# Attention in half-precision pairs, with transposing DMAs for x and the gate weights

## What is computed

```python
def xattn(query, key, value, w_q, w_k, w_v, w_o):      # 16 heads of 64
    q, k, v = (split_heads(a @ w) for a, w in ((query, w_q), (key, w_k), (value, w_v)))
    scores = einsum('bhqd,bhkd->bhqk', q, k) * 64 ** -0.5
    scores = scores + (1.0 - mask) * -10000.0           # k_pos <= q_pos
    weights = softmax(scores)
    return merge_heads(einsum('bhqk,bhkd->bhqd', weights, v)) @ w_o

def ffn(x, w_gate, w_up, w_down):       # qdq: round to 16 bits, lpbq: to 4 bits in blocks of 32
    x = qdq(x)
    up, gate = qdq(x @ lpbq(w_up).T), qdq(x @ lpbq(w_gate).T)
    o = qdq(qdq(gate * qdq_u16(sigmoid(gate))) * up)
    return o @ lpbq(w_down).T

x = x + tanh(g_xattn) * xattn(layernorm(x), ctx, ctx, ...)
x = x + tanh(g_ffn) * ffn(layernorm(x), ...)
```

## Time and profile before

| | |
|---|---|
| median of the runs | 1377.19 us |
| profiled execution | 1376.84 us |
| its span (first to last instruction) | 1375.1 us |
| PE busy | 1267.9 us (92%) |
| DVE busy | 1008.5 us (73%) |
| ACT busy | 663.6 us (48%) |
| POOL busy | 238.4 us (17%) |

### The profile page before, as it was taken

The page is one execution under the profiler, slowest core; times in us unless marked ns, Lnnn a source line. Parts: engine busy times, 40 slices in busy tenths (PEclk is TensorE's granted clock), DMA queues, the critical chain, the costliest instruction groups (busy, mean ns, idle before and its releaser), DMA issues. The chain is left out here.

```text
span 1375.1 us, 19079 instructions
## 1 busy us (share of the span) xinstructions
PE 1267.9 (92%) x6157; PEld 754.2 (55%) x6157; DVE 1008.5 (73%) x1465; ACT 663.6 (48%) x782; POOL 238.4 (17%) x331
## 2 busy tenths in 40 slices
PE   7999999999999999999999999999990069999998
PEld 6778868878887864444444444444440024444443
DVE  0379778878967666777777499989999984555544
ACT  3434443343344224444443388857768973434331
POOL 1034324314423221111111032210210000000000
PEclk9999999999999999999999999999995579999999
DMA  8002212312212338776665799963377954545453
GB/s 335 2 24 96 82 46 85 99 38 77 92 69 69 103 135 253 223 225 217 214 214 164 237 323 339 332 226 138 130 259 296 322 193 133 181 154 185 157 171 112
DMA packets 126475, 231.95 MB, mean 169 GB/s; under 512 B 38352, under 2 KB 50640, under 8 KB 126416
## 3 DMA queue, kind: packets, MB, share of 16 engines
q1 hardware_dynamic: 126128, 231.26, 49.9%
q10 hardware_dynamic: 288, 0.00, 0.0%
HBM read 136.32 MB, written 91.23 MB: 165 GB/s over the span
## 5 line engine op out<-in xcount | busy, mean ns | idle before, releaser
L1799 PE MATMUL pD<-Wh,xph 128*128 128x512 f16 x384 | 145.5, 379 | 1.0 <-DVE xpl L1774 1.0
L1276 PE MATMUL gpG<-xph,Wh 128*128 128x512 f16 x384 | 145.8, 380 | 0.2 <-DVE xpl L1198 0.2
L1276 PE MATMUL gpG<-xpl,Wh 128*128 128x512 f16 x384 | 145.8, 380 | 0.0
L1276 PE MATMUL gpG<-xph,Wl 128*128 128x512 f16 x384 | 145.8, 380 | 0.0
L1276 PE MATMUL pU<-xph,Wh 128*128 128x512 f16 x384 | 145.5, 379 | 0.0
L1276 PE MATMUL pU<-xpl,Wh 128*128 128x512 f16 x384 | 145.5, 379 | 0.0
L1276 PE MATMUL pU<-xph,Wl 128*128 128x512 f16 x384 | 145.5, 379 | 0.0
L1799 PE MATMUL pD<-Wl,xph 128*128 128x512 f16 x384 | 145.5, 379 | 0.0
L1799 PE MATMUL pD<-Wh,xpl 128*128 128x512 f16 x384 | 145.5, 379 | 0.0
L1181 ACT ACTIVATE gst<-gpG,rw 128x512 f32<-128x512 f32 x96 | 65.8, 686 | 148.1 <-PE gpG L1276 144.4
L1211 DVE TENSOR_REDUCE gmx<-gst 128x512 f32 (+1 forms) x96 | 65.5, 682 | 61.9 <-ACT gst L1181 61.7
(11 more groups left out here) (223 smaller groups left out, 2608.9 us busy)
## 6 DMA issues: line engine op xcount, KB each, us to landing
dub<-up_d SPq DMA_DIRECT2D x42, 768.0 KB, 4.8
gate_d<-gst SPq DMA_DIRECT2D x96, 256.0 KB, 2.6
gb<-gate_d SPq DMA_DIRECT2D x24, 768.0 KB, 7.1
up_d<-ust SPq DMA_DIRECT2D x72, 256.0 KB, 5.3
eu<-up_d SPq DMA_DIRECT2D x22, 768.0 KB, 6.4
xr<-xn_d SPq DMA_DIRECT2D x9, 1024.0 KB, 6.5
xin<-in_x SPq DMA_DIRECT2D x32, 256.0 KB, 2.8
x_d<-x SPq DMA_DIRECT2D x32, 256.0 KB, 2.0
```

The costliest lines, as they stand in the source:

```text
L1276: mm = pe.matmul(ps[:, :], Ws[:, it, kt * P:(kt + 1) * P], xs[:, kt, :], start=(kt == 0 and Ws is Wh and xs is xh), stop=(kt == KT - 1 and ...
L1799: mm = pe.matmul(pD[4 * t + q][:, :], os_[n][:, cs], Ws[:, it, :], start=(it == 0 and os_ is oh and Ws is Wh), stop=(it == IT - 1 and os_ ...
```

## The change

All halves of attention become float16 in place of fp32r: xh, xl, Ah, Al, pTh, pTl, Vh, Vl. To stay in float16's range each operand is scaled: x by 2^10 and p by 2^14 with constants, A and V by factors from bounds that are computed once (the largest absolute values of w_q and kT, of w_o and vT, spread over the partitions by TensorE, `spread_bounds`, and worked on by VectorE in `fit_a` and `fit_v`); the factors are taken out again in the exp and in the residual.

x is no longer turned by TensorE. ACT rounds the normalised rows into nh, GpSimd subtracts into nl, and SP turns both by transposing DMAs into xh and xl, of which there are now four each, two steps before they are used. The gate weight jobs go the same way: ACT rounds the dequantised tile, GpSimd subtracts, SP turns both halves, and stores them one step later.

```diff
         xin = [sb(ph, f"xin{n}", [P, H], F32) for n in range(BQ)]
         xn = [sb(ph, f"xn{n}", [P, H], F32) for n in range(2)]
-        xh = [sb(ph, f"xh{n}", [P, H], F32R) for n in range(2)]
-        xl = [sb(ph, f"xl{n}", [P, H], F32R) for n in range(2)]
+        nh = [sb(ph, f"nh{n}", [P, H], F16) for n in range(2)]
+        nl = [sb(ph, f"nl{n}", [P, H], F16) for n in range(2)]
+        xh = [sb(ph, f"xh{n}", [P, H], F16) for n in range(4)]
+        xl = [sb(ph, f"xl{n}", [P, H], F16) for n in range(4)]
...
# SP, step
+                if have(k + 2):
+                    j = k + 2
+                    sp.wait_ge(*tile(xl_done, b, j))
+                    sp.sem_inc(J.apart, 1)
+                    sp.wait_ge(*tile(s_ps, b, j - 4))
+                    sp.sem_inc(J.apart, 1)
+                    for part_, to in ((nh, xh), (nl, xl)):
+                        sp.dma_start_transpose(blocks_of(to[j % 4]), part_[j % 2][:, :]).then_inc(xt_in[j % 2], 16)
+                q = job_at(k, jobs, 3)
+                if q is not None:
+                    dsts = job_dst(b, q)
+                    sp.wait_ge(*at(turn_in[q % 2], 16 * JB * b, 32 * (q // 2) + 32))
+                    sp.sem_inc(J.apart, 1)
+                    for part_, dst in zip(turned[q % 2], dsts):
+                        sp.dma_start(dst, part_[:, :]).then_inc(J.stored[q % 2], 16)
                 q = job_at(k, jobs, 2)
                 if q is not None:
-                    job_store(sp, J, b, q, job_dst(b, q))
+                    sp.wait_ge(*at(J.lo_done, JB * b, q + 1))
+                    sp.sem_inc(J.apart, 1)
+                    sp.wait_ge(*at(J.stored[q % 2], 16 * JB * b, 32 * (q // 2)))
+                    sp.sem_inc(J.apart, 1)
+                    for part_, to in zip((J.hi[q % 2], J.lo[q % 2]), turned[q % 2]):
+                        sp.dma_start_transpose(blocks_of(to), part_[:, :]).then_inc(turn_in[q % 2], 16)
                 q = job_at(k, jobs, 1)
                 if q is not None:
                     job_load(sp, J, b, q + J.NJ, job_src(b, q + J.NJ))
...
# GpSimd, step
+                q = job_at(k, jobs, 2)
+                if q is not None:
+                    n = q % J.NJ
+                    pool.wait_ge(*at(J.hi_done, JB * b, q + 1))
+                    pool.wait_ge(*at(turn_in[n], 16 * JB * b, 32 * (q // 2)))
+                    pool.tensor_tensor(J.lo[n][:, :], J.d[n][:, :], J.hi[n][:, :], ALU.subtract).then_inc(J.lo_done, 1)
                 if have(k - 1):
...
+                if have(k + 2):
+                    j = k + 2
+                    pool.wait_ge(*tile(xh_done, b, j))
+                    pool.wait_ge(*used(b, j))
+                    pool.tensor_tensor(nl[j % 2][:, :], xn[j % 2][:, :], nh[j % 2][:, :], ALU.subtract).then_inc(xl_done, 1)
...
# VectorE, step
                         for h, cs in enumerate(halves):
                             dve.wait_ge(*part(pTh_done, b, j, h))
-                            dve.tensor_tensor(pTl[:, cs], pT[:, cs], pTh[:, cs].bitcast(F32), ALU.subtract).then_inc(pTl_done, 1)
+                            dve.scalar_tensor_tensor(out=pTl[:, cs], in0=pT[:, cs], scalar=P_TOP, in1=pTh[:, cs],
+                                                     op0=ALU.mult, op1=ALU.subtract).then_inc(pTl_done, 1)
...
-                if have(k + 1):
-                    j = k + 1
-                    dve.wait_ge(*tile(xh_done, b, j))
-                    dve.wait_ge(*tile(s_ps, b, j - 2))
-                    dve.tensor_tensor(xl[j % 2][:, :], pX[:, :], xh[j % 2][:, :].bitcast(F32), ALU.subtract).then_inc(xl_done, 1)
...
+            for r in range(2):
+                dve.wait_ge(wq_in[r], 16)
+            largest_of(0, flat(wq))
             for j in range(2):
                 statistics(0, j)
+            dve.wait_ge(k_sb, ROUNDS)
+            largest_of(1, flat(kT))
+            dve.wait_ge(id_set, 2)
+            fit_a()
+            dve.wait_ge(wo_in, 16)
+            largest_of(2, flat(wo))
             schedule(dve, step, straight=True)
...
# TensorE
             def scores(b, k):
-                pe.wait_ge(*tile(xl_done, b, k))
+                pe.wait_ge(*at(xt_in[k % 2], 16 * BQ * b, 32 * (k // 2) + 32))
...
-                        for kt in range(KT):
-                            mm = pe.transpose(pX[:, kt * P:(kt + 1) * P], xn[j % 2][:, kt * P:(kt + 1) * P], ident[:, :])
-                        mm.then_inc(xT_ps, 1)
...
-                q = job_at(k, jobs, 1)
-                if q is not None:
-
-                    pe.wait_ge(*tile(xl_done, b, k + 1))
-                    job_turn(pe, J, b, q, ident)
```

More of the change, by code:

```diff
@@ L189 @@
 ROUNDS = 4
+X_TOP, P_TOP, M_TOP = 2.0 ** 10, 2.0 ** 14, 2.0 ** 15
 def four_tiles(xn_d, T):
@@ L412, in front_phase @@
         srec = sb(ph, "srec", [P, 2, HEADS], F32)
+        bounds = sb(ph, "bounds", [P, 4], F32)
+        wide = sb(ph, "wide", [P, 4], F32)
+        fit = sb(ph, "fit", [P, 16], F32)
+        (A_TOP, A_T, A_UNIT, A_INV, A_SCALE, S_UNIT, S_SCALE, V_TOP, V_T, V_UNIT, V_INV, V_SCALE, V_BACK, O_SCALE) = (
+            fit[:, n:n + 1] for n in range(14))
         pT = pb(ph, "pT", 1024)
@@ L417, in front_phase @@
         x1_out, x2_out, gate_stored = front_out
-        J = Jobs(mk, ph, "pj", JB, 2, [pX], gate_stored)
+        J = Jobs(mk, ph, "pj", JB, 2, None, gate_stored)
+        turned = [[sb(ph, f"pj{part}T{n}", [P, 512], F16) for part in ("hi", "lo")] for n in range(2)]
+        turn_in = [sem(f"pj_turn_in{n}", 32) for n in range(2)]
+        xt_in = [sem(f"xt_in{n}", 32) for n in range(2)]
         with ExitStack() as early:
@@ L443, in front_phase @@
         kbd_set, vb_set = sem("kbd_set"), sem("vb_set")
+        bound_done, bound_ps, fit_link, a_fit, v_fit = (sem(n) for n in ("bound", "bound_ps", "fit_link", "a_fit", "v_fit"))
         apart_p, apart_e = sem("apart_p"), sem("apart_e")
@@ L616, in normal, with high_rows @@
                 act.activation(to[n][:, :], src[:, :], ACT.Identity, bias=rs_[:, n, 2:3], scale=rs_[:, n, 1:2]).then_inc(done, 1)
+            def high_rows(b, j):
+                act.wait_ge(*tile(xn_done, b, j))
+                act.wait_ge(*used(b, j))
+                act.activation(nh[j % 2][:, :], xn[j % 2][:, :], ACT.Copy).then_inc(xh_done, 1)
             def step(b, k, have, jobs):
@@ L622, in step @@
                     of_batch(act, vT, vb, b + 1, vb_set)
-                q = job_at(k, jobs, 2)
-                if q is not None and which == 0:
-                    job_hi(act, J, b, q)
                 if have(k - 2):
@@ L630, in step @@
                         act.wait_ge(*part(pT_ps, b, j, h))
-                        act.activation(pTh[:, cs], pT[:, cs], ACT.Copy).then_inc(pTh_done, 1)
-                if q is not None and which != 0:
-                    job_hi(act, J, b, q)
+                        act.activation(pTh[:, cs], pT[:, cs], ACT.Copy, scale=P_TOP).then_inc(pTh_done, 1)
                 def chunk_high(n):
                     act.wait_ge(*at(ch_ps, NCH * b, NCH * ahead + 8 * which + n + 1))
+                    if not jobs and b == 0 and ahead == 0 and n == 0:
+                        act.wait_ge(v_fit if which else a_fit, 1)
                     if which == 0:
-                        act.activation(Ah[:, n // 2, halves[n % 2]], bank_of(k, 0, n), ACT.Copy, scale=SCALE).then_inc(ch_hi, 1)
+                        act.activation(Ah[:, n // 2, halves[n % 2]], bank_of(k, 0, n), ACT.Copy, scale=A_SCALE).then_inc(ch_hi, 1)
                     else:
-                        act.activation(Vh[:, block_of(n), :], bank_of(k, 1, n), ACT.Copy).then_inc(ch_hi, 1)
+                        act.activation(Vh[:, block_of(n), :], bank_of(k, 1, n), ACT.Copy, scale=V_SCALE).then_inc(ch_hi, 1)
                 early_highs = 2 if which == 0 and have(k - 2) else 0
@@ L654, in exponentials @@
                         act.wait_ge(*tile(sub_done, b, j))
-                        act.activation(pr[j % 2][:, :], pr[j % 2][:, :], ACT.Exp).then_inc(exp_done, 1)
+                        act.activation(pr[j % 2][:, :], pr[j % 2][:, :], ACT.Exp, scale=S_UNIT).then_inc(exp_done, 1)
                 def high():
-                    if have(k + 1):
-                        j = k + 1
-                        act.wait_ge(*tile(xT_ps, b, j))
-                        act.wait_ge(*tile(s_ps, b, j - 2))
-                        act.activation(xh[j % 2][:, :], pX[:, :], ACT.Copy).then_inc(xh_done, 1)
+                    if have(k + 2) and k + 2 >= 2:
+                        high_rows(b, k + 2)
+                    q = job_at(k, jobs, 1)
+                    if q is not None:
+                        n = q % J.NJ
+                        act.wait_ge(*at(J.deq_done, JB * b, q + 1))
+                        act.wait_ge(*at(turn_in[n], 16 * JB * b, 32 * (q // 2)))
+                        act.activation(J.hi[n][:, :], J.d[n][:, :], ACT.Copy).then_inc(J.hi_done, 1)
                 def normal2():
@@ L814, in normal @@
```

(16 more changed lines are left out.)

101 lines of the change are left out of this document (70 added, 31 removed).

## The result

The changed kernel takes 1364.84 us (median of 4 runs, 1361.4 to 1366.12) against 1376.93 beside it: ratio 0.991, 95% interval 0.9892 to 0.9927. It is faster by 12.1 us, where 28.6 were forecast; 1364.8 lies in the range, near its end. The execution that was profiled is the quickest of the four: 1361.4 us, span 1359.2.

A forecast was written before the change was run, and what follows sets the result against it. TensorE was taken as the bound, with VectorE full in job steps. Gains of 22.8 us in three job batches, 4.9 in the last, 0.9 before the first and 0 at the start sum to 28.6: 1349 us, range 1334 to 1366.

The forecast's parts named there:

- The plain step: A last-batch step (one tile of 128 rows) without weight jobs: from 12.42 to 11.45 us, not TensorE's own 11.2.
- the loop through the softmax: Chain from TensorE's start through ACT, VectorE and GpSimd's product to the next step's transposes: 11.4 us, not shortened.
- rival 2: GpSimd's subtraction of half-precision data nearer 1.9 us than 1.05, about 3 us a batch more: 1357 us, chance 0.17.
- the load's wait: VectorE waits 2 us, once in a batch, for job 3's weight tile, whose load SP issues later behind DMA transposes.
- steps 3 to 7: Tiles of 128 rows in a batch with weight jobs: 64.05 to 61.1 us, a gain of 3.0 a batch.
- the start: New reductions and small VectorE operations before the first steps: taken as 0, between a gain of 1 and a loss of 3.
- Steps 8, 9, 10: Last three steps of a job batch: step 8 gains 2.0 us, steps 9 and 10 together 2.6, their softmax loop having room.
- eight re-entries: Step 8: first matmul behind each fp32 product of A gets 0.1 us quicker, 0.7 in all.
- Steps with jobs: VectorE is the one that is full: VectorE works 13.17 us without pause, more than TensorE's 12.84; low halves leave it, so 12.0 in steps 4 to 6.
- rival 3: DMA transposes slow in traffic, both halves 10.5 us instead of 3.7, some 15 us back: 1363 us, chance 0.10.
- Rival 1: TensorE stays the only bound, as if VectorE, GpSimd and SP had room: gain 46, 1331 us, chance 0.12.
- Rivals 2, 4 and 5: 4: transposes landing past 10 us, slower, 1401 us, chance 0.05. 5: time goes elsewhere, nothing left, 1377, 0.04.

The follow-up runs named there:

- e6: Changed kernel with VectorE's residual ahead of the scores' maximum and subtraction in steps 3 to 6, its statistics behind the subtraction: 1357.36 us.
- e10: Changed kernel with the next weight tile's load ahead of x's transposes, ScalarE's output tile ahead of the weight's high half, and e6's order: 1348.39 us.
- e9: Changed kernel with all five moves: early load, output tile first, residual first with statistics last, block maxima in PSUM, tile 2's statistics earlier: 1337.08 us.
- e2: Changed kernel with SyncE issuing the load of the next weight tile ahead of x's transposes instead of behind them: 1357.31 us.
- e3: Changed kernel with the weight tile's block maxima kept in PSUM instead of SBUF: 1358.77 us.
- e11: Changed kernel with the early load of e2, ScalarE's output tile ahead of the weight's high half, and the block maxima of e3: 1348.56 us.
- e5: Changed kernel with the weight tiles turned by TensorE as before; half precision and x's turn by DMA stay: 1365.14 us.
- e4: Half precision alone: changed kernel with x and weights turned by TensorE as before and VectorE making the low halves from PSUM: 1365.77 us.
- e7: Changed kernel with tile 2's statistics on VectorE before the reduction of the last weights at the start: 1357.99 us.
- e12: Changed kernel with early load and output tile first, plus x's DMA transposes issued twice, the first pair into tiles nobody reads: 1360.35 us.
- e1: The changed kernel run again without any edit: 1362.92 us.

## Why the gain was less than half of the forecast

**What came as forecast.** TensorE: a half-precision matmul every 0.216 us, no turns. The plain step: 11.54 against 11.45, and the loop through the softmax sets it: with 0.9 us of VectorE taken from the loop (e6) it is 11.23, TensorE's own 11.2. The 0.09 over are the exp's, 1.15 us with its scale read from a tile, 1.06 before; an edit that I took at nothing. The last batch 4.7 against 4.9. The turns: 1.20 and 1.25 us of SP, landed in 2.5. GpSimd's subtraction 1.16 against 1.05, far from rival 2's 1.9; the load's wait 2.74 against 2.

**Where it went.** In the profiled execution 12.8 of the 28.6 us are missing: 5.1 in steps 9 and 10, 4.1 in steps 3 to 7, 2.2 in step 8 (each in three batches) and 1.4 at the start; the rest cancels. The median lacks 3.7 more, which no trace of its execution shows.

**The step that failed most: "Steps 8, 9, 10".** They hold 7.3 of the 12.8. Steps 9 and 10, forecast 28.2, were 29.9. "Their softmax loop has room in 8 and 9, and is met within 0.3 us in 10" was wrong in 9. Behind VectorE's subtraction comes ScalarE's exp, behind that its high half of V, behind that VectorE's low half, and for this TensorE waits 0.77 us (404.15). With the statistics out of that chain (e6, e10) the wait is gone and step 9 takes 15.72 instead of 16.56. Step 10 lost to something that the prediction didn't ask for, TensorE's wait of 0.49 us for the residual (415.74); without it (e6, e10) the step takes 12.86 instead of 13.34, and the two steps together 28.58. The other wait of step 10, 1.22 us for a low half of V, is 1.21 in e10 and is no part of this gain.

Step 8, 18.67 against 18.0, is the 0.7 for eight re-entries, a bound of 0 to 1.2 a batch of which the whole was taken. e9 has no pause in step 8, and 18.67 still. The matmuls of A in the kernel before, then in e9:

```profile
272.94 1.05 PE L891 MATMUL pT<-kbd,wqT 128*128 128x128 f32 x8
273.74 0.48 PE L925 MATMUL pO<-Vh,pTh 128*128 128x512 f32 x1
274.06 0.41 PE L925 MATMUL pO<-Vl,pTh 128*128 128x512 f32 x1
```

```profile
355.11 1.05 PE L1007 MATMUL pT<-kbd,wqT 128*128 128x128 f32 x8
356.00 0.38 PE L1041 MATMUL pO<-Vh,pTh 128*128 128x512 f16 x1
356.21 0.38 PE L1041 MATMUL pO<-Vl,pTh 128*128 128x512 f16 x1
```

The re-entry did come, 0.21 us to the next matmul instead of 0.32, but the eight products ahead of it take 0.89 instead of 0.80, and give it back. That term was put at nothing.

**"Steps with jobs: VectorE is the one that is full": the wrong reason, and near the right number by luck.** It took VectorE's 13.17 us for work, and each 0.6 taken from it for a gain. The earlier trace rows has no pause, but an instruction that is held counts as busy. The scaling had 0.85 us before, for a job that it does in 0.17 when nothing holds it. In the changed kernel it took 1.44 in steps 3 and 4, and VectorE's steps were 11.94 and 12.82 in the third batch (forecast 11.4 and 12.0); in 5 and 6, where GpSimd's new low half moved the product behind the scaling, it took 0.17 to 0.32, and VectorE's steps without the load's wait (e2) are 11.63 (forecast 12.0). What two steps lost the other two gained: the four take 48.0 us against 47.4. So against the forecast the held time cost little; what it could have given is 4 us, as e3 and e11 show. e5 shows the exchange one for one.

**The load** was the larger part of what steps 3 to 7 lost. With the load early (e2) they take 59.2, 59.8 and 59.5 us, against the forecast's 59.1 without the load's wait; in the changed kernel 61.8, 63.6 and 62.0. So the wait cost 2.6, 3.8 and 2.6 where 2 were forecast, the 3.8 in the batch where the clock fell behind the pause at 254.71. The prediction named "everything behind it in its order" behind the wait, and didn't follow it to TensorE: VectorE's residual stands there, and TensorE's value matmuls wait for residuals for 13 us in 12 places, 0.7 us before.

**The start**, forecast 0 between -1 and 3, cost 1.4. The new reductions (4.42 and 2.27 us against 4.8 and 2.4) come before tile 2's statistics, whose normalisation stands on ScalarE in front of A's first halves. e4 has the same late start (76.53) without any DMA turn: it belongs to the bounds. e7 gets 5.0 to 6.0 us of it back.

**Two ends of the sum.** Before the experiments the change read as half precision plus turns by DMA. e4 and e5 say which part paid: by the ratios, 10.7 of 14.0 us are half precision; the turn of x by DMA added 0.5 and the weights' turn 2.8, neither more than these runs can tell from nothing.

**The rivals.** The time is closest to rival 3 (1363), and its mechanism is not there: transposes land in 2.5 us and doubling them leaves plain steps alone (e12). Rival 1 (1331, TensorE alone) is what e9 nearly reaches with 1337. Rivals 2, 4 and 5 are out.

**Still open.** Whether an instruction of VectorE with its source in PSUM is never held: beside the scaling, seven pairs of `pTl` (1.25 us) and four maxima of `pS` (1.21 to 1.22) that began in the middle of a long GpSimd instruction took no longer than elsewhere (1.25 to 1.29, 1.21 to 1.23), but no run tried it on purpose with others. What is left of the spread of the changed kernel's runs (5 us), since only two of its executions have a trace. That the clock falls behind some pauses (2.24 us at 254.71) and not behind others as long (2.23 at 143.70, 2.15 at 366.61, 2.53 at 145.25 in e1) was seen and not explained.

## What to carry to other kernels

An engine without a pause may still be held: look for an instruction that takes several times what its size asks, and compare its end with the end of what GpSimd does beside it, before you count on time that you take from it. For each instruction that a change delays, write down who waits for it on every engine, through the buffers that are reused too (a residual in the only bank, a high half until its transposes have read it), not only along the path you suspect. When several waits of 1 to 3 us appear, mend them one at a time on the chip: here five moves of a few lines gave 24 us, where the change itself had given 12 to 14.

## What the chip showed unexpectedly

- VectorE's scaling of 128x16 with source and destination in SBUF took 1.44 or 0.85 us beside GpSimd's product and ended with it, within 0.04 us; beside it a reciprocal of the same size (0.25) and a reduction of it (0.11) were not held, and with the source in PSUM the scaling took 0.17.
- The other way round, GpSimd's 128x1 product took 0.60 us instead of 0.19 beside VectorE's dequantisation, which has two inputs in SBUF, and ended within 0.05 us of it (before at 248.10, changed at 341.80).
- The price of TensorE's pauses is more than their length. The 3.1 us that the pause in front of A lost in e7 brought step 2 forward by 5.0 to 6.0 us.
- Eight fp32 products of A take 0.89 us between half-precision matmuls, 0.80 to 0.82 between fp32r ones, and the matmul behind them 0.22 us instead of 0.32.
- Reading a scale from a tile instead of a constant made ScalarE's 128x1024 exp 1.15 us instead of 1.06, and its 128x512 copy 0.68 to 0.69 instead of 0.59 to 0.60.
